# Constant products in five waits of TensorE, in a two-layer graph attention kernel

## The reference

```
h = max(layernorm(x), 0)
q, k, v = heads(h @ Wq + bq), heads(h @ Wk + bk), heads(h @ Wv + bv)
scores  = q @ k.T / sqrt(64) + where(adj, 0, -9e15)
ctx     = softmax(scores) @ v
x       = x + (ctx @ Wf + bf)
```

## Time and profile before

| | us |
|---|---|
| median of three runs | 1850.08 |
| lowest and highest run | 1849.11, 1852.0 |
| profiled execution | 1853.11 |
| its span in the trace | 1851.3 |
| TensorE busy | 1821.8 (98% of the span) |
| VectorE busy | 1621.9 (88%) |
| ScalarE busy | 1561.2 (84%) |
| mean granted clock of TensorE | 0.995 of full |

### The profile page before, as it was taken

How to read it: one execution, slowest core, us unless ns; L and a number is a source line. 1 busy time by engine, 2 the same in 40 slices (tenths; PEclk the granted TensorE clock), 3 DMA queues, 4 the chain that set the end, 5 groups by cost and what they waited for, 6 DMA issues and landing times.

```text
span 1851.3 us, 54324 instructions
## 1 busy us (share of the span) xinstructions
PE 1821.8 (98%) x17210; PEld 1050.4 (57%) x17210; DVE 1621.9 (88%) x5551; ACT 1561.2 (84%) x4793; POOL 1490.9 (81%) x1781
## 2 busy tenths in 40 slices
PE   7899999999999999999999999999999999999998
PEld 3455555555555555555555555555555555555555
DVE  7889898898988988889888888988889888898876
ACT  5888888888888888888888888888888888888884
POOL 4678888888888888888888888888888888888761
PEclk8999999999999999999999999999999999999999
DMA  6656666666666666666667666667666666666655
GB/s 195 175 171 185 204 205 193 197 205 199 208 197 199 200 193 209 205 197 194 193 207 203 203 196 200 201 199 215 195 196 194 198 207 197 200 179 193 194 169 180
DMA packets 439942, 363.32 MB, mean 196 GB/s; under 512 B 207700, under 2 KB 406888, under 8 KB 439656
## 3 DMA queue, kind: packets, MB, share of 16 engines
q1 hardware_dynamic: 439656, 359.86, 65.1%
HBM read 184.30 MB, written 175.37 MB: 194 GB/s over the span
## 4 chain that ended last, share of the span: by engine, by line
PE 86%; DVE 4%; DMA 3%; SPq 3%; issue 2%; ACT 1%; POOL 1%; DVEq 0%; ACTq 0%; POOLq 0%
PE ps_qk L683 12%; PE ps_shared L683 12%; PE ps_shared L685 12%; PE ps_shared L684 12%; PE ps_qk L684 12%; PE ps_qk L685 12%; PE ps_shared L780 7%; PE ps_scores L800 7%; SPq L375 2%; DMA p_dram<-p_blocks 1%; DVE probs L1316 1%; DMA p_moved<-p_dram 1%; DVE qk_lo L1296 1%; POOL probs L551 1%; ACT probs L1013 1%
## 5 line engine op out<-in xcount | busy, mean ns | idle before, releaser
L1013 ACT ACTIVATE probs<-probs,row_min 128x128 f32<-128x128 f32 x1512 | 583.1, 391 | 2.5 <-DVE row_rcp L1281 1.5
L551 POOL TENSOR_TENSOR probs<-probs,row_rcp 128x768 f32<-128x768 f32 x252 | 370.2, 1469 | 215.5 <-DVE row_rcp L1281 215.2
L1316 DVE CUSTOM_DVE_ANT_0 probs<-ps_scores,mask,minus_scale 128x128 f32<-128x128 f32 x1512 | 429.6, 347 | 0.9 <-issue 0.6
L568 POOL TENSOR_TENSOR p_half<-p_moved,p_half 128x768 f16<-128x768 f32 x236 | 388.0, 1644 | 1.6 <-ACT p_half L988 1.6
L1296 DVE SCALAR_TENSOR_TENSOR qk_lo<-ps_qk,qk_bias,qk_hi 128x512 f16<-128x512 f32 x384 | 278.7, 747 | 77.2 <-ACT qk_hi L996 76.1
L1013 ACT ACTIVATION_READ_ACCUMULATOR probs<-probs,row_min 128x1 f32 x1512 | 288.8, 191 | 0.0
L996 ACT ACTIVATE qk_hi<-ps_qk,qk_bias 128x512 f16<-128x512 f32 x384 | 258.1, 672 | 14.6 <-PE ps_qk L685 14.6
L547 POOL TENSOR_TENSOR x_tile<-x_tile,out_bias 128x384 f32<-128x384 f32 x256 | 257.7, 1007 | 1.1 <-DVE out_bias L1240 1.1
L1327 DVE SCALAR_TENSOR_TENSOR x_tile<-ps_shared,out_scale,x_tile 128x384 f32<-128x384 f32 x256 | 157.1, 613 | 111.2 <-PE ps_shared L685 108.6
L683 PE MATMUL ps_shared<-wf_hi,ct_hi 128*128 128x384 f16 x768 | 250.6, 326 | 2.4 <-DVE ct_lo L1290 2.4
L685 PE MATMUL ps_shared<-wf_hi,ct_lo 128*128 128x384 f16 x768 | 250.8, 327 | 0.0
(11 more groups left out here) (152 smaller groups left out, 3997.7 us busy)
## 6 DMA issues: line engine op xcount, KB each, us to landing
p_dram<-p_blocks SPq DMA_DIRECT2D x256, 384.0 KB, 2.4
p_moved<-p_dram SPq DMA_DIRECT2D x1008, 96.0 KB, 2.4
h_dram<-h_blocks SPq DMA_DIRECT2D x252, 192.0 KB, 2.6
h_moved<-h_dram SPq DMA_DIRECT2D x1008, 48.0 KB, 2.0
x_tile<-in_x SPq DMA_DIRECT2D x128, 192.0 KB, 2.9
out_x<-x_tile SPq DMA_DIRECT2D x128, 192.0 KB, 2.7
adj_u<-in_adj SPq DMA_DIRECT2D x64, 64.0 KB, 2.6
p_half<-p_dram SPq DMA_DIRECT2D x16, 96.0 KB, 2.3
```

The lines of the kernel that those rows point to most:

```text
L551: nc.gpsimd.tensor_tensor(probs_of(t, i), probs_of(t, i), row_rcp[i % 2][:, :].rearrange("p (a o) -> p a o", o=1) .to_broadcast([P, HEADS, ...
L568: nc.gpsimd.tensor_tensor(p_part(i, 1), p_moved[i % 2][:, :, :].rearrange("p a n -> p (a n)"), p_part(i, 0), ALU.subtract).then_inc(p_set, 1)
L1013: ins = nc.scalar.activation(tile[:, s, :], tile[:, s, :], ACT.Exp, bias=row_min[i % 2][:, s:s + 1], scale=-1.0, accum_out=row_sum[i % 2][ ...
L1316: ins = nc.vector.tensor_tensor_reduce(tile[:, s, :], score_bank(i, s // PAIRS)[:, (s % PAIRS) * P:(s % PAIRS + 1) * P], mask[b][:, i, :], ...
```

## The change

`keep_busy` takes the bank to write as an argument. Products are added in five places of TensorE's list, 24 in all:

- four between `share_value_peak` and `turn_first(1)`
- two between `turn_first(2)` and `turn_first(3)`
- five between `turn_first(3)` and `turn_largest(0)`
- six in `score(1, 0)`, into the bank ps_scores0 that the scores will overwrite, between its two waits; for this the wait on `masked` is moved ahead of that on `qk_set`, in every `score`
- seven between `output(A, 0)` and `output(A, 1)`, into ps_qk1

```diff
-            def keep_busy(products):
+            def keep_busy(products, free=ps_shared[0]):
                 for _ in range(products):
-                    pe.matmul(ps_shared[0][:, :], idle_work[:, 0:P], idle_work[:, :], start=True, stop=True)
+                    pe.matmul(free[:, :], idle_work[:, 0:P], idle_work[:, :], start=True, stop=True)
...
             def score(t, i):
                 b = unit_no(t) % 2
+                wait(pe, masked, unit_count(t, PER, i - 1))
+                if (t, i) == (1, 0):
+                    keep_busy(6, score_bank(i, 0))
                 if i == 0:
                     pe.wait_ge(qk_set, unit_count(t, CHUNKS, CHUNKS))
                 if (t, i) == (0, 0):
                     pe.wait_ge(scales_set, 1)
                     pe.wait_ge(out_bias_set, 1)
-                wait(pe, masked, unit_count(t, PER, i - 1))
...
                 output(A, 0)
+                keep_busy(7, ps_qk[1])
                 output(A, 1)
...
             turn_first(0)
             share_value_peak()
+            keep_busy(4)
             turn_first(1)
             keep_busy(2)
             turn_first(2)
+            keep_busy(2)
             turn_first(3)
+            keep_busy(5)
             turn_largest(0)
             project_v(0, 0)
```

## The result

The changed kernel takes 1846.65 us (median of 14 runs, 1845.01 to 1848.98) and the kernel before 1850.02 (14 runs, 1849.03 to 1852.0): ratio 0.9982, 95% interval 0.9974 to 0.9991, so 3.4 us less, between 1.7 and 4.8. The forecast was 1.9 us less. The profiled execution of the changed kernel took 1845.01, the lowest of its runs, with a span of 1843.2.

What follows compares the result with a forecast made beforehand. TensorE was taken to bound the kernel (86% of the chain), with half-clock falls to remove. Gains of 0.8 + 0.9 + 1.5 = 3.2 us on the profiled execution, scaled to 1.9 for the median, gave 1848.2 us, range 1845.8 to 1851.5.

Steps and rivals of the forecast that it cites:

- The products are free: All five places: added products fit TensorE's waits, costing the path 0, at most 0.5 us.
- From one execution to the median: Whole kernel: runs differ by how many falls they have, so the profile's 3.2 us becomes 1.9 in the median.
- its two bounds: Changed median: 1849.1 if the lowest run had no falls, 1846.9 if all three runs had all.
- The start: First V projections at full clock, scales up to 1.3 us earlier; gain 0.8 us, bounds 0 and 1.3.
- the bound that the prediction named: Start: upper bound of 1.3 us on the gain, VectorE's wait of 1.30 us for the shared maximum.
- The middle: Unit 1's first scores: without the fall the q products no longer run at double price; gain 0.9 us, bounds 0 and 0.9.
- The last units: Between unit A's outputs: fall costing 1.7 us is gone, nearly all goes through; gain 1.5 us, bounds 0.8 and 1.7.
- The start keeps its fall: Start: clock returns only where it does now, start gives 0, median falls 1.4 to 1848.7 us; chance 0.18.
- the two cases that have a held clock there: Start: the forecast case, gain 1 to 3.5 us, chance 0.42, and more than the trace, chance 0.11.
- Nothing arrives: All places: clock falls as before or a DMA takes the time back; 1850.1 us, 1849 to 1851.5; chance 0.24.
- More than the trace shows: Start: half clock lasts beyond 19.84 in other runs, start gives 2.2 us, time 1845.5; chance 0.11.
- Slower: Loop: earlier entry makes TensorE wait in each of 61 slots, 3.7 us, 1853.8 with no gain; chance 0.05.

Runs made afterwards that it cites:

- the two clean traces: Profiled executions without a TensorE wait in the loop: the unchanged kernel before, run again, and the changed kernel; spans 1846.1 and 1843.2 us.
- eighteen: Changed kernel with eighteen products instead of five ahead of the largest weights; 1847.03 us, ratio 0.9984 to the kernel before.
- before again: The kernel before, unchanged, measured and profiled once more; 1849.69 us, ratio 1.0003, profiled execution 1847.91 us.
- last only: Kernel before plus only the seven products between the outputs of unit A, with the moved wait on `masked`; 1849.81 us, ratio 1.0003.
- middle only: Kernel before plus only the six products ahead of unit 1's first scores, with the moved wait on `masked`; 1849.67 us, ratio 1.0.
- the one without the last part: Changed kernel without the seven products in the last units, keeping start and middle; 1847.09 us, ratio 0.9984 to the kernel before.
- The start alone: Kernel before plus only the eleven products of the start, with the moved wait on `masked`; 1849.45 us, ratio 0.9997.

## Why the prediction was right or wrong

The measured time lies inside the range, and its direction and mechanism were right: of the 2.9 us between the two clean traces, 3.0 lie in the three legs with a fall. The size, 1.9 us, was too small against 3.4, 2.3 and, over all runs with a clock (25 and 110), 1846.84 against 1849.92, 3.1 us. The prediction took 3.7 us as the least that can be told from no change; the intervals reached 1.6 us to each side.

**The products are free.** Right. All five groups fit in their waits at full clock; the group of five also at half clock (2.34 us against 2.35 worked out). The price of an overrun, measured with eighteen at unit 1's scores, is nearly the overrun itself.

**From one execution to the median.** This step failed. It read the 3.0 us between the profiled execution and the median as falls that the other runs did not have, and so scaled 3.2 to 1.9 (the middle of its two bounds, 1849.1 and 1846.9, is 1848.0 and not 1848.2). The row that said otherwise stood in the earlier trace rows: 3.1 us of waits in the loop, that are in neither the kernel before run again nor the changed kernel's first trace. The clock of the runs, 0.994 to 0.996 in 86 of 110, says that the falls are in most of them. Unscaled, 1850.0 - 3.2 = 1846.8, 0.2 from the measured median; that it comes so near is in part luck, as the start was sized too low and the other two terms too high.

**The start.** Term 0.8, measured 1.6, between 1.0 (before again) and 2.2 (last only), and 1.6 in the medians when it is left out. The first 0.75 was right: `sum_out_bias` starts 7.81 us after the largest weights and not 8.56. What was cut too short is what follows. VectorE's 1.3 us reach unit 0's first scores, where TensorE waited 1.09 us on qk_lo and now 0.67, and unit 1's scores keep it: 52.33 - 51.06 = 1.27, the bound that the prediction named. Two traces pass the bound: "middle only", with a fall of 13.7 us, by 0.8, and "last only", with one no longer than in the earlier trace rows, by 0.9; why is open.

**The middle.** Term 0.9, measured 0.7 in the trace of before. The wait on GpSimd's ht_lo grew from 0.39 to 0.91, as `apply_probs(0, 0)` ended earlier, so up to the q products nothing is gained (3.62 and 3.61 us from unit 1's scores), as forecast. The twelve q products gave 0.87, and 0.15 of it went into a gap ahead of unit 2's V products, which the term had left out. In the median the six products can't be told from none.

**The last units.** Term 1.5, measured 1.36 in the pair of clean traces. The fall is not in every run without the products (it is absent in the one without the last part), so a mean gain is below it. The DMA of the last probabilities does not keep the gain, but its own lateness, up to 1.9 us in a wait, hides it in the "last only" trace.

**The rivals.** "The start keeps its fall" happened in one of the five traces that have exactly these eleven products (the one without the last part), and there only from 17.25 on. The Trainium skill's rule that transpositions do not count ("TensorE: Matmul & The Clock Gate", Part 4, PE-mode transpose) is not contradicted: with products among them the clock held, without the first two groups it fell at 10.25. No run with transpositions alone in place of the products tests it. The prediction calls this rival likelier than a held clock at the start, but gives it 0.18, against 0.53 for the two cases that have a held clock there; four of the five traces held it. "Nothing arrives" is excluded by both intervals. "More than the trace shows" was partly so: falls of 13.7 us at the start exist. "Slower" did not come: TensorE's waits in the loop were 0 to 3.5 us in all traces, in no order with the change.

What stays open: whether a fall that is prevented in one place makes another longer or moves it. Two traces look so (the fall of 7.0 us without the middle's products, the one at 17.25 without the last's), and none can decide it. The start alone gave 0.4 us in the median, where its leg in the trace is 1.0 and 1.2 shorter than in the two traces of the kernel before. The interval (1.7 us to each side) holds both, so whether the parts add exactly isn't settled. Seven of the 110 runs of the kernel before show a clock of 1.000, yet their median, 1848.1, is 1.3 above the changed kernel's; and the ten with 0.999, which by the legs should be lower too, are not (1850.1). No trace of such a run was taken, so some 1.3 us of the 3.1 may have a cause other than the clock.

## What to carry to other kernels

Here a fall of TensorE's clock cost time where it reached into dense work that others waited for, so look at the windows around each wait near 2 us, and price the half-clock stretch by the matmuls in it and by who waits behind them. Before scaling one trace to a median, split the difference: waits on late transfers in the loop and falls of the clock are different terms, and the clock of each run tells whether the second are there. Constant products in a wait were free up to its length. Some wait can be left over, but not without risk: with 1.7 to 2.3 us left ahead of the largest weights, one of five traces still had a late fall.

## What the hardware showed unexpectedly

The same kernel, profiled twice with the same falls, differed by 5.2 us in its span. A fall also came among dense V products, near 17.25, some 0.7 us after the wait had ended, with the wait 2.13 us long behind the five products. An empty wait of 2.35 us was followed by a fall in three traces (near 1821.5 twice, at 1825.5 once) and by none in two others. The one of 2.4 us at unit 1's scores, where nothing fills it, was followed by a fall in four traces and by none in one.
